# fp16 parts in place of fp32r parts in the expert matmuls of a cross-attention and soft-mixture-of-experts kernel

## The reference

```python
x = x + xattn(layernorm(x), ctx, ctx, mask, wq, bq, wk, bk, wv, bv, wo, bo)
h = layernorm(layernorm(x)) * norm_g + norm_b            # 16 x 100 x 256
logits = einsum('bnd,esd->bnes', h, layernorm(slot_embeds) * slot_g + slot_b)
dispatch = softmax(logits, axis=1)                        # over the tokens
combine = softmax(logits.reshape(B, N, E*S), axis=-1)     # over all slots
slots = einsum('bnd,bnes->besd', h, dispatch)
gate = gelu(einsum('besd,edf->besf', slots, Wg) + bg)     # F = 512
up = einsum('besd,edf->besf', slots, Wu) + bu
eout = einsum('besf,efo->beso', gate * up, Wd) + bd
x = x + einsum('bns,bso->bno', combine, eout)
```

## Time and profile before

| | us |
|---|---|
| median of 3 runs | 1165.66 |
| lowest and highest | 1162.25, 1166.73 |
| the profiled execution | 1163.88 |
| its span in the trace | 1162.2 |
| PE, PEld, DVE, ACT, POOL busy | 1063.1, 869.9, 698.5, 576.3, 332.6 |
| granted TensorE clock, mean | 0.958 |

### The profile page before, as it was taken

One profiled execution on the slowest core, in us unless ns is written; L12 is line 12 of the kernel. 1 busy time (PEld: TensorE's weight loads), 2 busy tenths in 40 slices (PEclk: granted clock), 3 DMA queues, 4 the chain that ended last, 5 costly groups with the idle time before them and its releaser, 6 DMA issues.

```text
span 1162.2 us, 22171 instructions
## 1 busy us (share of the span) xinstructions
PE 1063.1 (91%) x7172; PEld 869.9 (75%) x7172; DVE 698.5 (60%) x1247; ACT 576.3 (50%) x1084; POOL 332.6 (29%) x348
## 2 busy tenths in 40 slices
PE   5688999999877888789999999999999999999997
PEld 3466777777663444478888888888888888888885
DVE  5556777777636888544555555655645555556544
ACT  2376878778655788733433343433424334333421
POOL 5267767667664343210010010100100100100000
PEclk8789999999958999889999999999999999999998
DMA  8858778678403534432142242432331331422123
GB/s 208 183 120 142 168 156 159 155 140 172 88 2 96 145 99 112 122 129 65 41 132 75 56 117 74 107 103 76 113 92 41 113 93 41 131 74 54 47 57 83
DMA packets 115080, 121.50 MB, mean 105 GB/s; under 512 B 46633, under 2 KB 105445, under 8 KB 115029
## 3 DMA queue, kind: packets, MB, share of 16 engines
q1 hardware_dynamic: 100908, 79.07, 30.5%
q0 software_dynamic: 10960, 40.67, 11.5%
q10 hardware_dynamic: 3160, 1.11, 0.6%
HBM read 73.87 MB, written 29.93 MB: 89 GB/s over the span
## 4 chain that ended last, share of the span: by engine, by line
PE 55%; DVE 1%; issue 1%; ACT 0%; DVEq 0%; ACTq 0%
PE down L1579 16%; PE gate L1539 15%; PE up L1539 15%; PE mix L1519 5%; PE mix L1512 4%; DVE gate_sb L1430 0%; ACT hid_h L1490 0%; DVE hid_l L1435 0%; DVE wd_l L1441 0%; DVE x L1415 0%; ACT gate_sb L1486 0%; DVE slot_l L1406 0%; DVEq L1633 0%; DVEq L1429 0%; DVEq L1412 0%
## 5 line engine op out<-in xcount | busy, mean ns | idle before, releaser
L1486 ACT ACTIVATE gate_sb<-gate,bgu 128x512 f32<-128x512 f32 x128 | 88.1, 689 | 222.3 <-PE gate L1539 207.7
L402 POOL TENSOR_TENSOR p_l<-p_f,p_h 121x800 f16<-121x800 f32 (+1 forms) x96 | 163.7, 1718 | 80.4 <-ACT p_h L652 79.5
L1490 ACT ACTIVATE hid_h<-gate_sb 128x512 fp32r<-128x512 f32 x128 | 80.9, 632 | 178.0 <-DVE gate_sb L1430 178.0
L1430 DVE SCALAR_TENSOR_TENSOR gate_sb<-up,bgu,gate_sb 128x512 f32<-128x512 f32 x128 | 95.9, 749 | 103.1 <-PE up L1539 101.3
L486 DVE TENSOR_REDUCE head_max<-at_rows 100x2 f32<-100x722 f32 x124 | 112.9, 910 | 71.8 <-PE at_rows L730 69.8
L1579 PE MATMUL down<-wd_h,hid_h 128*128 128x256 f32 x512 | 150.7, 294 | 0.7 <-DVE hid_l L1435 0.7
L1435 DVE TENSOR_TENSOR hid_l<-gate_sb,hid_h 128x512 fp32r<-128x512 f32 x128 | 88.6, 692 | 93.6 <-ACT hid_h L1490 93.6
L1579 PE MATMUL down<-wd_l,hid_h 128*128 128x256 f32 x512 | 144.8, 283 | 0.0
L1579 PE MATMUL down<-wd_h,hid_l 128*128 128x256 f32 x512 | 144.8, 283 | 0.0
L1263 POOL DMA_DIRECT2D wd<-in_Wd x16 | 12.2, 766 | 320.8 <-DVE eo L1453 300.4
L1579 PEld LDWEIGHTS down<-wd_h,hid_h 128*128 128x128 f32 x512 | 98.0, 191 | 3.4 <-issue 1.0
(11 more groups left out here) (165 smaller groups left out, 2279.1 us busy)
## 6 DMA issues: line engine op xcount, KB each, us to landing
eo_pair<-eo SPq DMA_DIRECT2D x128, 128.0 KB, 2.4
k_parts<-kq_n SPq DMA_DIRECT2D x16, 724.0 KB, 3.7
kt<-k_parts SPq DMA_DIRECT2D x32, 362.0 KB
wgu<-in_Wg POOLq DMA_DIRECT2D x16, 512.0 KB, 6.2
wgu<-in_Wu POOLq DMA_DIRECT2D x16, 512.0 KB, 6.9
wd<-in_Wd POOLq DMA_DIRECT2D x16, 512.0 KB, 5.2
combine<-combT SPq DMA_DIRECT2D x16, 400.0 KB, 4.0
dispatch<-dispT SPq DMA_DIRECT2D x16, 400.0 KB
```

Source lines behind the costliest of these rows:

```text
L402: nc.gpsimd.tensor_tensor(p_l[i][0:kn, :, 0:N], p_f[i][0:kn], p_h[i][0:kn, :, 0:N], ALU.subtract).then_inc(p_low, 1)
L1430: nc.vector.scalar_tensor_tensor(gate[c % 2][:], up_ps[c % 2][:], bu_col(bgu, pair, e, c), gate[c % 2][:], ALU.add, ALU.mult).then_inc(hid ...
L1486: nc.scalar.activation(gate[c % 2][:], gate_ps[c % 2][:], ACT.Gelu, bias=bg_col(bgu, pair, e, c)).then_inc(gelu_ready, 1)
L1490: nc.scalar.activation(hid_h[:, c, :], gate[c % 2][:], ACT.Copy).then_inc(hidh_ready, 1)
```

## The change

The parts of all operands of the gate, up and down matmuls (wgu, wd, slots, hidden) become fp16 in place of fp32r: still three products each, the same shapes and the same number. fp16 has a small range, so everything is scaled by powers of two: the gate, up and down weights by a power of two from the largest absolute value of the expert's tensor, the hidden values by one from a bound, the normalised input (through norm_g and norm_b) by one of its own. Scales are undone in gelu (un_gate), in the up bias (bu_s) and in eo (un_down).

The new work that this needs:

- Maxima: per expert DVE reduces (tensor_reduce, in max_of) wgu (128x2048), wd (128x1024) and the biases to one value per partition. SP stores the 128 rows to DRAM and loads them back broadcast to all partitions (share_hidden, share_down, two transfers one after the other). DVE then makes the scales in a chain of small operations, each of which waits for the one before (hidden_scales: 11 instructions, down_scales: 5).
- For pair 0 this is done at the end of the attention phase. SP loads Wd of both experts into the slot tile and Wg and Wu of both into the tile of x (six transfers of 512 KB), DVE takes the maxima at the end of step B-1 and the scales at the end of step B+1. At the end of step B-2 it scales norm_g and norm_b (norm_scaled, 10 instructions). The loading of bgu goes from POOL in routing to SP in attention.
- For the next pair, the maxima are taken in the down stages, beside the eo steps: wgu of expert 0 at the end of unit (h0, e0), wgu of expert 1 between the two eo of (h0, e1), the biases and wd of expert 0 after them, the gate and up scales before the eo of (h1, e0), wd of expert 1 after them, the down scales at the end of (h1, e1).

What is moved:

- in a chunk, slot_l or the combine add stands between DVE's two steps (gate_sb and hid_l), and slot_h stands before hid_h on ACT;
- wgu_h of the next pair's expert 0: into chunk 0 of (h1, e1); its wgu_l: from after both eo of (h1, e0) to between the two eo of (h1, e1); wgu_l of expert 1: from the end of (h1, e1) to after the chunks of the next pair's (h0, e0). For pair 0, expert 1 the split goes from routing into the first unit;
- on POOL, Wd of the next pair is loaded from within h0 (after wdl_ready), the first half of disp before the combine weights, the second after them.

At the start of the kernel three small memsets are added on POOL, and in attention several semaphores are merged; no matmul, copy or transfer there changes.

The diff, cut to its core:

```diff
+            if t == B - 3:
+                load_hidden_bias(sp, a, keep)
+                sp.wait_ge(seT_done, SC // 2)
+                for e in range(2):
+                    sp.dma_start(slot[:, FC * e:FC * e + FC, :], a["Wd"][e].rearrange("(c p) d -> p c d", p=P)).then_inc(first_in, 16)
+            if t == B - 2:
+                sp.wait_ge(dev_ready, B)
+                for e in range(2):
+                    for i, n in enumerate(("Wg", "Wu")):
+                        half = x_full[:, BH * e + 4 * i:BH * e + 4 * i + 4, :].rearrange("p b d -> p (b d)")
+                        sp.dma_start(half.rearrange("p (c f) -> p c f", c=2), a[n][e].rearrange("(c p) f -> p c f", p=P)).then_inc(first_in, 16)
+            if t == B + 1:
+                share_down(sp, keep, 0)
+                share_hidden(sp, keep, 0)
+        def norm_scaled():
...
+            for n in ("norm_g", "norm_b"):
+                nc.vector.tensor_scalar(keep[n][:], keep[n][:], s_x, None, ALU.mult).then_inc(norm_step, 1)
...
+                norm_scaled()
...
+                dve.wait_ge(first_in, 96)
+                for e in range(2):
+                    max_of(nc, keep["max_down"][:, e:e + 1], slot[:, FC * e:FC * e + FC, :].rearrange("p c d -> p (c d)"), keep["down_top"])
+                dve.wait_ge(keep["bias_in"], 32)
+                max_hidden_bias(nc, dve, keep, 0)
+                for e in range(2):
+                    max_of(nc, keep["max_hidden"][:, e:e + 1], x_full[:, BH * e:BH * e + BH, :].rearrange("p b d -> p (b d)"), keep["hidden_top"])
+            if t == B + 1:
+                hidden_scales(nc, dve, keep, 0)
+                down_scales(nc, dve, keep, 0)
...
-            if t == B:
-                weights_lo(nc, dve, keep, 1, 0)
...
-                if t == B - 1:
-                    weights_hi(nc, act, keep, 1, 0)
...
-        "wgu_h": [sb(f"wgu_h{e}", [P, 2, 2, F], F32R) for e in range(2)],
-        "wgu_l": [sb(f"wgu_l{e}", [P, 2, 2, F], F32R) for e in range(2)],
+        "wgu_h": [sb(f"wgu_h{e}", [P, 2, 2, F], F16) for e in range(2)],
+        "wgu_l": [sb(f"wgu_l{e}", [P, 2, 2, F], F16) for e in range(2)],
...
 def weights_lo(nc, dve, keep, e, pair):
     dve.wait_ge(keep["wh_ready"][e], pair + 1)
-    nc.vector.tensor_tensor(keep["wgu_l"][e][:], keep["wgu"][e][:], keep["wgu_h"][e][:].bitcast(F32), ALU.subtract).then_inc(keep["wl_ready"][e], 1)
+    dve.sem_inc(keep["waited"], 1)
+    nc.vector.scalar_tensor_tensor(keep["wgu_l"][e][:], keep["wgu"][e][:], keep["w_scale"][:, bass.ds(2 * pair + e, 1)], keep["wgu_h"][e][:],
+                                   ALU.mult, ALU.subtract).then_inc(keep["wl_ready"][e], 1)
...
+def share_hidden(eng, keep, pair):
+
+    eng.wait_ge(keep["hidden_top"], 3 * pair + 3)
+    eng.sem_inc(keep["waited"], 1)
+    eng.dma_start(keep["hidden_dram"].rearrange("(p j) -> p j", p=P), keep["max_hidden"][:]).then_inc(keep["hidden_moved"], 16)
+    eng.wait_ge(keep["hidden_moved"], 32 * pair + 16)
+    eng.sem_inc(keep["waited"], 1)
+    eng.dma_start(keep["all_hidden"][:, 0:4 * P], keep["hidden_dram"].partition_broadcast(P)).then_inc(keep["hidden_moved"], 16)
+
...
+def hidden_scales(nc, dve, keep, pair):
+    def made(n):
+        dve.wait_ge(step, SCALE_STEPS * pair + n)
+        dve.sem_inc(keep["waited"], 1)
+
+    dve.wait_ge(keep["hidden_moved"], 32 * pair + 32)
+    dve.sem_inc(keep["waited"], 1)
+    nc.vector.tensor_reduce(top[:, 0:4], keep["all_hidden"][:].rearrange("q (p j) -> q j p", j=4), AX.X, ALU.max).then_inc(step, 1)
+    made(1)
+    nc.vector.tensor_tensor(power.bitcast(I32), top[:, 0:2].bitcast(I32), bits, ALU.bitwise_and).then_inc(step, 1)
+    nc.vector.scalar_tensor_tensor(bound, top[:, 0:2], n256, top[:, 2:4], ALU.mult, ALU.add).then_inc(step, 1)
...
-    hid_h, hid_l = sb("hid_h", [P, FC, ROWS], F32R), sb("hid_l", [P, FC, ROWS], F32R)
+    hid_h, hid_l = sb("hid_h", [P, FC, ROWS], F16), sb("hid_l", [P, FC, ROWS], F16)
...
+                    if h == 0 and e == 1 and not last:
+                        share_hidden(sp, keep, pair + 1)
+                    if h == 1 and e == 0 and not last:
+                        share_down(sp, keep, pair + 1)
...
-                pool.wait_ge(slots_done, 4 * (2 * pair + 2))
+                pool.wait_ge(wdl_ready[0], pair + 1)
                 pool.sem_inc(waited, 1)
-                for h in range(2):
-                    hb = slice(BH * h, BH * h + BH)
-                    pool.dma_start(disp[:, hb], at(dispatch_dram, pair + 1)[:, hb]).then_inc(disp_in[h], 16)
+                load_down(pool, a, keep, 0, pair + 1)
+                load_slot_weights(pair + 1, 0, 4 * (2 * pair + 1))
+                pool.wait_ge(wdl_ready[1], pair + 1)
+                pool.sem_inc(waited, 1)
+                load_down(pool, a, keep, 1, pair + 1)
             if not first:
...
-                        dve.wait_ge(hidh_ready, FC * u + c + 1)
-                        if not (first and h == 0 and e == 0):
-                            dve.wait_ge(down_done, 2 * u)
-                        nc.vector.tensor_tensor(hid_l[:, c, :], gate[c % 2][:], hid_h[:, c, :].bitcast(F32), ALU.subtract).then_inc(hidl_ready, 1)
...
                         r = 2 * e + c // 2
                         if c % 2 == 0 and nxt:
                             dve.wait_ge(slots_done, 4 * (hs + 1) + r + 1)
                             slots_lo(hs + 1, 1 - h, r)
                         if c % 2 == 1 and prev:
                             combine_add(hs - 1, 1 - h, r, first)
+                        dve.wait_ge(hidh_ready, FC * u + c + 1)
+                        if not (first and h == 0 and e == 0):
+                            dve.wait_ge(down_done, 2 * u)
+                        dve.sem_inc(waited, 1)
+                        nc.vector.scalar_tensor_tensor(hid_l[:, c, :], gate[c % 2][:], keep["hid_scale"][:, bass.ds(ex, 1)], hid_h[:, c, :],
+                                                       ALU.mult, ALU.subtract).then_inc(hidl_ready, 1)
...
+                    if h == 0 and e == 0:
+                        weights_lo(nc, dve, keep, 1, pair)
+                    if h == 1 and e == 0 and not last:
+                        hidden_scales(nc, dve, keep, pair + 1)
                     for g in range(2):
...
-                        nc.vector.tensor_tensor(eo[e][:, 2 * g:2 * g + 2, :], down_ps[g][:],
-                                                bd[e][:].rearrange("p (o d) -> p o d", o=1).broadcast_to([P, 2, D]), ALU.add).then_inc(eo_ready, 1)
-                    if h == 1 and not last:
-                        weights_lo(nc, dve, keep, e, pair + 1)
+                        dve.wait_ge(keep["bd_in"][e], 16 * pair + 16)
+                        dve.sem_inc(waited, 1)
+                        nc.vector.scalar_tensor_tensor(eo[e][:, 2 * g:2 * g + 2, :], down_ps[g][:], keep["un_down"][:, bass.ds(ex, 1)],
+                                                       bd[e][:].rearrange("p (o d) -> p o d", o=1).broadcast_to([P, 2, D]),
+                                                       ALU.mult, ALU.add).then_inc(eo_ready, 1)
+                        if not last:
+                            if h == 0 and e == 0 and g == 1:
+                                max_gate_up(nc, dve, keep, 0, pair + 1)
+                            if h == 0 and e == 1 and g == 0:
+                                max_gate_up(nc, dve, keep, 1, pair + 1)
+                            if h == 0 and e == 1 and g == 1:
+                                max_hidden_bias(nc, dve, keep, pair + 1)
+                                max_down(nc, dve, keep, 0, pair + 1)
+                            if h == 1 and e == 0 and g == 1:
+                                max_down(nc, dve, keep, 1, pair + 1)
+                            if h == 1 and e == 1 and g == 0:
+                                weights_lo(nc, dve, keep, 0, pair + 1)
+                            if h == 1 and e == 1 and g == 1:
+                                down_scales(nc, dve, keep, pair + 1)
...
+                        if c % 2 == 0 and nxt:
+                            slots_hi(hs + 1, 1 - h, 2 * e + c // 2, first and h == 0)
...
-                            nc.scalar.activation(wd_h[e][:], wd[e][:], ACT.Copy).then_inc(wdh_ready[e], 1)
-                        if c % 2 == 0 and nxt:
-                            slots_hi(hs + 1, 1 - h, 2 * e + c // 2, first and h == 0)
-                    if h == 1 and not last:
+                            act.sem_inc(waited, 1)
+                            nc.scalar.activation(wd_h[e][:], wd[e][:], ACT.Copy,
+                                                 scale=keep["d_scale"][:, bass.ds(ex, 1)]).then_inc(wdh_ready[e], 1)
+                        if h == 1 and e == 1 and c == 0 and not last:
+                            act.wait_ge(up_done, FC * u)
+                            weights_hi(nc, act, keep, 0, pair + 1)
+                        if first and h == 0 and e == 0 and c == 2:
```

(4 more changed lines are left out.)

324 lines of the change are left out of this document (221 added, 103 removed).

## The result

The changed kernel takes 1176.17 us (median of 6 runs, 1172.05 to 1177.55), the kernel before 1165.0 us (6 runs) beside it: 1.0084 times as long, 95% interval 1.0063 to 1.0104. It is slower, by 0.6 to 1.0%, where I had forecast 1152. The profiled span is 1174.3 us, 12.1 us longer than before.

What follows compares the result with a forecast made beforehand. PE was taken to bound the expert phase, DVE the end of attention. -39.0 + 13.3 + 1.6 + 1.0 + 11.6 - 2.2 = -13.7 us gave 1152 against the median, own range 1143 to 1164, 8-in-10 range 1138 to 1172.

Steps and rivals of the forecast that it cites:

- the clock: PE's granted clock in the expert phase: no fall counted in the sum, falls left to a rival.
- The stream: Expert matmuls of 512 and 256 columns: fp16 cuts each one's surplus over its columns to 2.7 ns, -39.0 us.
- Rivals 2 and 3: Expert matmuls: surplus not a matter of type, 1191 (0.08; one shape 0.10); loads not hidden with 16-bit streams, 1223 (0.03).
- The wait at a pair's end: PE waits 1.9 us for DVE's wgu_l at the end of seven pairs, +13.3 us.
- Rival 1: Pair ends: the clock falls in the new wait, +2.5 us at 7 pairs, so 1170; chance 0.11, wholly or in part.
- around the wait PE is busy without a gap: Pair ends: the argument given against a clock fall in the new 1.9 us wait.
- The chunk's new order: Chunks of expert units: hid_l of chunk 3 about 0.1 us late at 16 units, +1.6 us; first unit +1.0 once.
- Chunk 3's gate_sb, add and hid_l follow: h0 units, DVE behind wd_l: these operations end 6.3 us after up 2, where the 18 down matmuls end at 4.3 + 1.97.
- Maxima and scales in down stages: DVE in the down stages: some 12 us of new work per pair falls where DVE idled, costed at nothing.
- gate_sb is 1.1 us late: Worst case (h0, e1): DVE's gate_sb 1.1 us late, but PE needs it over 3 us on, so no cost.
- The end of attention: Pair 0's maxima (6.8 us) stand ahead of o_sum and scales (4.8 us) after x, +11.6 us.
- The end of routing: DVE's wgu_l, last before the expert phase, goes from there, -2.2 us.

Runs made afterwards that it cites:

- before_fp16: The kernel before with weights, slots and hidden rows in fp16 in place of fp32r, old order, no scaling: 1128.39 us, 0.9687.
- half_wait: The changed kernel with wgu_l of the next pair's expert 0 split, half ahead of the first eo, half where it stood: 1159.37 us, 0.9951.
- lo_last: The changed kernel with wgu_l of the next pair's expert 0 behind both eo and the down scales of (h1, e1): 1203.25 us, 1.0335.
- small_maxima: The changed kernel with the four maxima of pair 0's weights at the end of attention taken over 64 columns: 1176.98 us, 1.0094.
- order_back: The changed kernel with the chunk's old order on DVE and ACT: 1214.62 us, 1.0436.
- dve_order_back: The changed kernel with the chunk's old order on DVE alone, ACT keeping slot_h ahead of hid_h: 1208.07 us, 1.036.
- fp16_new_order: The kernel before with fp16 parts, no scaling, and the changed kernel's order within a chunk: 1130.75 us, 0.970.
- lo_wd1: The changed kernel with the next pair's expert 0 wgu_l ahead of the first eo of (h1, e1), and wd_l in chunk 1 of h0 units: 1143.74 us, 0.9808.
- all4: The changed kernel with wgu_l ahead of the first eo, wd_l in chunk 1, pair 0's maxima in DVE's waits and its scales in routing: 1137.53 us, 0.9759.

## Why the prediction was wrong, point by point

Two steps of the prediction failed in their mechanism: the clock, put at nothing in the sum, and the h0 unit, put at 0.1 us by a row of operations that left out ACT's hid_h. The rest are sizes and scatter.

**The stream: right.** Forecast -39.0 us, measured -36.3 by before_fp16. 512 columns come every 216 ns, as worked out, and 256 columns every 109.2 (5.24 us for 48), where I had 109.4; in the changed kernel 48 take 5.32 to 5.33 us. The missing 2.7 us are thus not in the matmuls' distance: the 0.07 us that an h0 unit of before_fp16 takes more than an h1 unit make about 1 us of them, the rest isn't worked out. Rivals 2 and 3 are out. By the Trainium skill, "TensorE: Matmul & The Clock Gate", section "Wait — 56ns, not 53.3ns?", 512 columns take 215.7 ns; the trace agrees. The 81 ns that its section "Back-to-back issue gap" gives for 128 columns would be 28 ns over the columns; here, with a load before each matmul, 2.7 at 512 and 2.5 at 256.

**The wait at a pair's end: mechanism right, size short.** Forecast 7 x 1.9, measured 7 x 2.33 = 16.3 us. eo, wgu_l and the steps between them are each 0.05 to 0.07 us longer than in the earlier trace rows, and behind wgu_l come 0.25 to 0.30 us until PE starts and by the unit's length 0.16 more, where I allowed 0.2. The upper bound, 7 x 2.4, held.

**The clock: the step that failed first.** Rival 1 had the mechanism, at a chance of 0.11, against which I put "around the wait PE is busy without a gap". That was no argument: half_wait, the changed kernel and lo_last have the same busy surroundings, and the clock fell behind 0, 5 and 7 of seven waits of 1.1, 2.2 and 4.9 us. The wait's length alone doesn't settle it either: at 2.0 to 2.2 us it fell behind six of seven in small_maxima and order_back and behind two of seven in dve_order_back, and what decides between them stays open. Cost: 5 x 1.66 = 8.3 us. The forecast named 2.5 us for a fall; it was 1.7, since the clock came back after some 8 matmuls.

**The chunk's new order: wrong on both sides.** Forecast +0.1 us in 16 h0 units. In the unit at 696.72 up 2 ends at 706.24; wd_l ends 4.28 us later (forecast 4.2), but PE needs it at 4.19 and starts at 4.52; hid_l of chunk 3 is there for PE at 6.90, where I had 6.3. The step that failed is "Chunk 3's gate_sb, add and hid_l follow": hid_l does not follow the add, it waits for ACT's hid_h, which with a scale takes 0.72 us and not 0.63. And I compared ends with needs to 0.1 us while leaving out some 0.15 to 0.25 us between an end and the waiting engine's start. Cost: 14 x 0.66 = 9.2 us. It is the price of wd_l's place with the longer operations, not of the order alone: fp16_new_order has 0.04 us of it, and lo_wd1 takes 0.55 of the 0.66 away with the order unchanged. The rows (timeline of DVE):

```profile
709.24 1.28 DVE L1642 SCALAR_TENSOR_TENSOR wd_l<-wd,d_scale,wd_h 128x1024 f16<-128x1024 f32 x1
...
712.24 0.75 DVE L1634 SCALAR_TENSOR_TENSOR hid_l<-gate_sb,hid_scale,hid_h 128x512 f16<-128x512 f32 x1 [0.28 <-ACT hid_h L1707]
```

That the order was also what keeps the loaded DVE in step (38 us without it), I had not seen at all.

**Maxima and scales in down stages: the zero held, for a reason not given.** With the new order PE waits for none of them; with the old one the kernel that carries them, and the longer operations, is 32 to 38 us slower. "gate_sb is 1.1 us late" looked at gate_sb alone, not at the mix banks behind it in the same queue.

**The end of attention: +15.6 us, forecast +11.6.** The maxima stood for 6.7 us (359.92 - 340.93, less 12.27 before; forecast 6.8), the scales for 4.3 (forecast 4.8). Missed were 1.9 us of waiting for the shares: I gave them 4.8 us from the last maximum by the earlier trace rows, and they took 7.1. PE's steps between o_sum and x took 0.3 more. The other 2.4 us were there before any maximum (340.93 against 338.58) and are scatter: over the profiles with the same code up to there, that o_sum starts between 336.56 and 342.54.

**The end of routing: -4.95, forecast -2.2.** The last slot_l now ends 0.48 us before the first gate matmul, the 2.2 us as forecast. The rest is scatter as well: routing takes 140.3 us in this profile and 142.0 to 144.1 in the eight others with the same code in it, against 144.4 to 145.3 in the three with the old code.

**The sum.** Units 2 to 29 should change by 28 x -1.13 + 16.3 + 9.2 + 8.3 = +2.2 us, and did by +2.1. The first two, the last two and the tail make -0.6, the expert phase starts 10.7 later: 12.1 us, the difference of the spans. Against my sum of -13.7 that is 25.8 us: the clock +8.3, the h0 units +7.6, attention +4.0, the wait +3.0, the first two and last two units +2.9 (at 1.13 us a unit, and 1.0 more for the first, I had -3.5 there), the stream +2.8 (32 x 1.13 in place of 39.0), routing -2.8. The clock was a mechanism that I had priced and not believed.

## What to carry to other kernels

When a stream gets faster, list what the other engines do in each unit and set it against the new, shorter unit, with 0.15 to 0.25 us for each hand-over: slack of 0.1 us is none. A wait put in front of a dense PE stream can cost more than its length: here 2.2 us did five times in seven, 1.1 us never. So a 2.3 us operation is worth moving by one place to where its engine waits anyway. And an order may be the price of one thing and the cure of another: test it with and without the load that came with it.

## What the hardware showed that I had not expected

- Behind a wait of PE in an otherwise dense stream, the granted clock fell from 2.4 to 1.2 GHz in none of seven cases at 0.9 to 1.1 us (half_wait), in all seven at 4.8 to 5.0 us (lo_last), and at 2.0 to 2.2 us in five of seven (the changed kernel), six (small_maxima), six (order_back) and two (dve_order_back). A fall cost 1.7 us at 2.2 us of wait and up to 2.1 at 5. Waits of 2.16 us came out on both sides within one execution; behind this one nothing slowed (chain of the changed kernel; compare the one at 675.14 above):

```profile
757.13 1.46 PE gate L1763 x6
758.59 1.29 PE up L1763 x6
```

- A slow clock can be free: at the start of the expert phase, twelve matmuls at 1.2 GHz took 5.28 us in the changed kernel, and PE did not wait for disp; in the six profiles with full clock there it waited 1.7 to 3.1 us for that transfer (4.6 us in all4, 5.9 in small_maxima).
- A scale from SBUF made ACT's and DVE's operations longer: gelu 771 ns in place of 689, hid_h 719 in place of 632, eo 748 in place of 692 on average (eo with SCALAR_TENSOR_TENSOR in place of TENSOR_TENSOR). Types did not: in before_fp16, without a scale, hid_h took 629 ns and hid_l 692, as before.
- A store of 128 maxima to DRAM and the broadcast load behind it took 7 us (from the last maximum at 360.0 to `top` at 367.09), and 8.1 in small_maxima (issue at 356.26, `top` at 364.36), where one transfer like them in the earlier trace rows had 2.4.
